# A residual with a conditioned relu layer: W loaded in rows of 4p + k over 128 partitions, x turned in columns 4p + k, W3 ahead of W2, and two instructions moved up

## The chip, the cores and the metric

The kernel runs on one core of one Trainium2 chip. The metric is the device time of one execution in microseconds. The kernel before took 111.57 us (median of three runs, 110.3 to 112.86).

## The reference

x is (4, 1024, 512) in float32, cond is (4, 256), W is (1536, 512), b is (512). Cut to what matters:

```
hidden = concatenate([cond, cond], axis=-1)                  # (4, 512)
x_mean = mean(x, axis=1)                                     # (4, 1, 512)
fused  = concatenate([x, x_mean, hidden], axis=-1)           # along the features, each row
out    = x + relu(fused @ W + b)
```

So with W cut into W1, W2, W3 of 512 rows each, out = x + relu(x @ W1 + bias of the batch), and that bias is mean(x) @ W2 + hidden @ W3 + b.

## The kernel before

**Data.** x is cut into eight groups g of 512 rows (two a batch). A group lies in `xa` with partition 32 j + m for row 32 lb + m and column quadrant j (128 columns). VectorE turns 32 x 32 blocks: `turn_x` (L288) takes the 32 columns 32 k to 32 k + 31 of each quadrant and writes block k of x transposed to a PSUM bank, 128 features by 512 rows. Partition 32 j + m of block k then holds feature 128 j + 32 k + m, and so W1's and W2's rows are loaded in that order, by one DMA for each 32 partitions.

**Three products for float32.** Each operand is split in two: ScalarE's `x_high` (L229) writes the rounded `xh` (and sums it over the rows into `xsum` in the same instruction), VectorE's `x_low` (L300) subtracts it from the PSUM bank to give `xl`. `w1_high` (L225, ScalarE) and the loop at L198 (POOL) do the same for W1, giving `w1h` and `w1l`. TensorE adds w1h xh, w1h xl and w1l xh over the four blocks k. A tile (g, t) is one quarter t of the output features for one group: 12 products of 512 columns into one of four PSUM banks `ps_y`. `n` numbers the tiles. Two banks `ps_xt` hold turned pieces, so `turn_x(n)` waits for `x_low(n - 2)`.

**Group 0** is done in two halves of 256 rows, block by block, as W1 lands. Its and group 1's products are copied by ScalarE's `save` (L237) to `relu_t`, since no bias is there yet.

**The bias.** `mean_terms(b)` (L317, VectorE) adds the sums of the two groups and makes `w2x`, W2's four blocks each times its part of the sum: one multiplication (L328), three multiply-adds (L331). `mean_bias(b)` (L421, TensorE) sums `w2x` over partitions into `ps_mean`. `sum_bias(b)` (L341, VectorE) adds the constant row and turns it into `bias`. The constant comes from `w3sum` on POOL (L210), 8 small products (two records each in the trace, L471), and `const_row` (L372).

**Output.** ScalarE's `relu(n)` (L242) adds the bias and applies relu, VectorE's `turn_back(n)` (L306) turns it into `back`, POOL adds it to `xa` (`residual`, L204), SP stores the group (L190). The last group is added by VectorE in half tiles.

**Orders written out by hand.** Each engine's list is in program order. ScalarE: `x_high(0)`, `x_high(1)`, `w1_high(0)`, `w1_high(1)`, then pairs, `x_high` to piece 10, `save(0)`, `x_high(11)`, more saves; and from relu 8 on, one `x_high` behind each relu. VectorE: group 1 and 2 are turned and split, `mean_terms(0)`, the constant row, `sum_bias(0)`, group 3, `mean_terms(1)`, then for each tile n its `turn_back(n)`, and from n = 4 on a `turn_x` and an `x_low` of the group three ahead. TensorE: group 0, tiles (1, 0) to (1, 3), constant, `mean_bias(0)`, tiles (2, 0) to (2, 3) with `mean_bias(1)` in the middle of (2, 3), then a loop over pairs of groups with the next `mean_bias` behind t = 2 of the second.

**Queues.** SP issues nearly all DMAs in order; ScalarE issues half of those of x's first group and of W1, at the start. In SP's list the order is: x's group 0 first half (two of four), W1 block 0, block 1, blocks 2 and 3 (two DMAs each), x's group 0 second half (two), cond (four), x's groups 1 and 2, W2 (four), W3 (two), b (four), then x's groups 3 to 7.

Of the kernel before, what the change touches and what calls it, by code (L numbers as in the profile page):

```python
# [24 lines left out]
P = 128  # L25
Q = 32
NQ = P // Q
# [5 lines left out]
XT_BANKS = 2  # L33
# [7 lines left out]
def build(nc, x, cond, w, bvec, out):  # L41
# [7 lines left out]
    assert D == NK * P and D == NQ * NK * Q and H == 2 and w.shape == (3 * D, D) and 2 * C == D  # L49
    assert NK % XT_BANKS == 0 and NK == Y_BANKS == BACK_RING and RELU_RING == H * NK  # L50

# [22 lines left out]
    ov = out.rearrange("b (h lb lm) (j e) -> (b h) j lm lb e", h=H, lm=Q, j=NQ)  # L74
    wv = w[0:2 * D, :].rearrange("(s j k m) o -> s j m k o", s=2, j=NQ, m=Q)

# [9 lines left out]
    with ExitStack() as ctx:  # L86
# [62 lines left out]

        def load_w1(eng, first, end, quadrants):  # L150
            for j in quadrants:
                eng.dma_start(w1[Q * j:Q * j + Q, first:end], wv[0, j, :, first:end]).then_inc(w1_landed[first], 16)  # L152

        def load_w2(eng, quadrants):
            for j in quadrants:
                eng.dma_start(w2[Q * j:Q * j + Q], wv[1, j]).then_inc(w2_landed, 16)

# [10 lines left out]
        @block.sync  # L168
        def _(sp):
            load_x0(sp, 0, LOW)  # L170
            load_w1(sp, 0, 1, LOW)
            load_w1(sp, 1, 2, LOW)
            load_w1(sp, 2, NK, LOW)
            load_x0(sp, 1, LOW)
            sp.wait_ge(cond_zeroed, 1)
            for j in range(NQ):
                sp.dma_start(cond_c[Q * j:Q * j + B], cv[j].rearrange("b (m k) -> b m k", k=CK)).then_inc(cond_landed, 16)  # L177
            load_x(sp, 1, ORDER)
            load_x(sp, 2, ORDER)
            load_w2(sp, ORDER)  # L180
            for r in range(2):
                sp.dma_start(w3[:, r], w3v[r]).then_inc(w3_landed, 16)
            for j in range(NQ):
                sp.dma_start(b_row[Q * j:Q * j + Q], bvec[P * j:P * j + P].partition_broadcast(Q)).then_inc(b_landed, 16)
            for g in range(3, G):
                load_x(sp, g, ORDER)
            for g in range(LAST):
                sp.wait_ge(added, NK * (g + 1))
                for j in ORDER:
                    sp.dma_start(ov[g, j], xa[Q * j:Q * j + Q, g]).then_inc(stored, 16)  # L190
            store_last(sp, range(0, 2))
            sp.wait_ge(stored, 16 * (NQ * LAST + 2 * NQ))

        @block.gpsimd
        def _(pool):
            nc.gpsimd.memset(cond_c[:], 0.0).then_inc(cond_zeroed, 1)

            for k in range(NK):  # L198
                pool.wait_ge(w1_landed[min(k, NK - 2)], 16 * NQ)
                pool.wait_ge(w1h_ready, k + 1)  # L200
                nc.gpsimd.tensor_tensor(as_tiles(w1l[:, k]), by_tile(w1[:, k]), as_tiles(w1h[:, k]),  # L201
                                        ALU.subtract).then_inc(w1l_ready, 1)
# [13 lines left out]
        def _(act):  # L216
            load_x0(act, 0, HIGH)
            act.wait_ge(ones_set, 1)
            nc.scalar.activation(act_warm[:], ones[:, 0:1], ACT.Relu)
            load_w1(act, 0, 1, HIGH)  # L220
            load_w1(act, 1, 2, HIGH)
            load_w1(act, 2, NK, HIGH)
            load_x0(act, 1, HIGH)

            def w1_high(k):  # L225
                act.wait_ge(w1_landed[min(k, NK - 2)], 16 * NQ)
                nc.scalar.activation(as_tiles(w1h[:, k]), by_tile(w1[:, k]), ACT.Copy).then_inc(w1h_ready, 1)  # L227
# [26 lines left out]

            x_high(0)
            x_high(1)
            w1_high(0)
            w1_high(1)
            for k in range(2, NK):
                x_high(k)  # L260
                w1_high(k)
            for n in range(NK, pieces_to(H) - 1):
                x_high(n)
            save(0)
            x_high(pieces_to(H) - 1)
            for n in range(1, NK):
# [19 lines left out]
        def _(dve):  # L286

            def turn_x(n):  # L288
                g, l, nl, k = pieces[n]
                if k == 0:  # L290
                    if g == 0:
                        dve.wait_ge(x0_landed[l // HL], 16 * NQ)
                    else:
                        dve.wait_ge(x_landed[g], 16 * NQ)
                if n >= XT_BANKS:
                    dve.wait_ge(xl_ready, n + 1 - XT_BANKS)
                nc.vector.transpose(ps_xt[:, n % XT_BANKS, 0:nl],  # L297
                                    xa[:, g, l // Q:(l + nl) // Q, Q * k:Q * k + Q]).then_inc(xt_ready, 1)

# [17 lines left out]
            def mean_terms(b):  # L317

                if b == 0:
                    nc.vector.tensor_tensor(xsum[:, 1], xsum[:, 0], xsum[:, 1], ALU.add).then_inc(halves_summed, 1)  # L320
                    dve.wait_ge(w2_landed, 16 * NQ)
                    dve.wait_ge(halves_summed, 1)
# [56 lines left out]
            for n, (g, l, nl, t) in enumerate(tiles):  # L379

                if n % NK == 0 and l == 0:
                    if n // NK % H == H - 1 and n // NK // H + 1 < B - 1:
                        sum_bias(n // NK // H + 1)
                    elif n // NK == H * (B - 1):
                        sum_bias(B - 1)
                turn_back(n)
# [145 lines left out]
```

## Time and profile before

| | us |
|---|---|
| median of three runs | 111.57 |
| the profiled execution | 109.98 |
| its span | 108.2 |
| PE busy | 97.4 |
| DVE (VectorE) busy | 85.4 |
| ACT (ScalarE) busy | 50.4 |
| POOL busy | 43.5 |

The granted TensorE clock was 0.996 of full speed over the span. The span runs from the first to the last instruction or transfer; the profiled execution's time has 1.8 us more around it. Times in the rows are in microseconds from the start of the span. An instruction's busy time may overlap the next one's, since engines pipeline. The idle time in brackets is that of the engine just before the instruction, with what ended it. DMA moved 20.08 MB, 186 GB/s in the mean.

### The profile page before, as it was taken

How to read it: one execution, taken by the hardware profiler on the slowest of the kernel's cores; microseconds unless marked ns; L12 is line 12 of the kernel's file. 1: busy time of each engine (PE TensorE's matmuls, PEld its weight loads, DVE VectorE, ACT ScalarE, POOL GpSimd, SP SyncE). 2: the span in 40 equal slices, each digit the busy share in tenths (PEclk: the TensorE clock that was granted, in tenths of full speed). 3: DMA queues.
4: the chain of work that ended last, by engine and by line, in shares of the span. 5: the costliest groups of instructions: out<-in, count | busy, mean ns of one | idle time of the engine just before them, and what ended most of it. 6: DMA issues, size and time to landing. Idle time of an engine off the chain costs nothing.

```text
span 108.2 us, 1750 instructions
## 1 busy us (share of the span) xinstructions
PE 97.4 (90%) x542; PEld 79.7 (74%) x542; DVE 85.4 (79%) x149; ACT 50.4 (47%) x122; POOL 43.5 (40%) x38
## 2 busy tenths in 40 slices
PE   5969999799969999489999999999999999999900
PEld 2349999688847886278888886888888868999900
DVE  1263869998997999999999955999999967796630
ACT  3185416985225991287396002873950008322210
POOL 1039500000440000999856400488564199960000
PEclk9999999999999999999999999999999999999998
DMA  2999999999999999999886194000861930969956
GB/s 71 276 291 264 227 226 230 243 250 333 220 220 222 222 222 222 226 224 263 244 204 186 33 236 126 0 0 0 210 178 41 241 106 0 217 181 230 245 126 171
DMA packets 35719, 20.08 MB, mean 186 GB/s; under 512 B 1536, under 2 KB 34432, under 8 KB 35712
## 3 DMA queue, kind: packets, MB, share of 16 engines
q1 hardware_dynamic: 33184, 18.42, 76.9%
q10 hardware_dynamic: 2528, 1.57, 5.4%
q8 instruction: 3, 0.05, 0.2%
q14 instruction: 4, 0.03, 0.1%
HBM read 11.60 MB, written 8.39 MB: 185 GB/s over the span
## 4 chain that ended last, share of the span: by engine, by line
PE 53%; DVE 18%; ACT 10%; DMA 7%; SPq 6%; issue 2%; ACTq 0%; DVEq 0%
PE ps_y L406 52%; DMA xa<-in_x_dram 7%; DVE w2x L331 6%; ACT xh L234 5%; ACT relu_t L252 3%; DVE ps_xt L297 3%; DVE xl L303 3%; DVE back L314 3%; SPq L152 2%; SPq L144 2%; ACT relu_t L239 1%; SPq L148 1%; SPq L177 1%; PE ps_mean L425 1%; DVE w2x L328 1%
## 5 line engine op out<-in xcount | busy, mean ns | idle before, releaser
L406 PE MATMUL ps_y<-xh,w1h 128*128 128x256 f32 (+2 forms) x160 | 52.9, 352 | 3.3 <-ACT relu_t L252 1.8
L406 PE MATMUL ps_y<-xl,w1h 128*128 128x256 f32 (+2 forms) x160 | 52.1, 347 | 0.0
L406 PE MATMUL ps_y<-xh,w1l 128*128 128x256 f32 (+2 forms) x160 | 51.9, 347 | 0.0
L206 POOL TENSOR_TENSOR xa<-xa,back 128x512 f32 x28 | 35.7, 1297 | 29.8 <-DVE back L314 29.8
L406 PEld LDWEIGHTS ps_y<-xh,w1h 128*128 128x128 f32 x160 | 28.7, 189 | 8.9 <-issue 3.2
L406 PEld LDWEIGHTS ps_y<-xh,w1l 128*128 128x128 f32 x160 | 28.7, 189 | 3.9
L406 PEld LDWEIGHTS ps_y<-xl,w1h 128*128 128x128 f32 x160 | 28.8, 189 | 3.6
L252 ACT ACTIVATE relu_t<-ps_y,bias 128x512 f32<-128x512 f32 (+1 forms) x28 | 17.3, 626 | 29.4 <-DVE bias L346 20.1
L234 ACT ACTIVATE xh<-ps_xt 128x512 fp32r<-128x512 f32 (+1 forms) x36 | 19.7, 548 | 14.9 <-DVE ps_xt L297 14.8
L297 DVE STREAM_TRANSPOSE ps_xt<-xa 128x512 f32<-128x512 f32 (+1 forms) x36 | 22.3, 642 | 5.1 <-DMA xa<-in_x_dram 4.7
L303 DVE TENSOR_TENSOR xl<-ps_xt,xh 128x512 fp32r<-128x512 f32 (+1 forms) x36 | 22.2, 617 | 4.6 <-ACT xh L234 4.6
L314 DVE STREAM_TRANSPOSE back<-relu_t 128x512 f32<-128x512 f32 (+1 forms) x36 | 22.1, 631 | 3.9 <-ACT relu_t L252 3.8
L331 DVE SCALAR_TENSOR_TENSOR w2x<-w,bsum,w2x 128x512 f32<-128x512 f32 x12 | 11.3, 938 | 0.4
L210 POOL TENSOR_TENSOR w3sum<-w 128x1024 f32<-128x1024 f32 x1 | 2.4, 2396 | 16.3 <-DMA w<-in_L_cond_W_dram 16.3
L201 POOL TENSOR_TENSOR w1l<-w,w1h 128x512 fp32r<-128x512 f32 x4 | 5.1, 1293 | 6.3 <-ACT w1h L227 6.2
L234 ACT ACTIVATION_READ_ACCUMULATOR xh<-ps_xt 128x1 f32 x36 | 7.1, 197 | 0.0
L252 ACT ACTIVATE relu_t<-relu_t,bias 128x512 f32<-128x512 f32 x8 | 5.4, 720 | 2.2 <-DVE bias L346 2.2
L239 ACT ACTIVATE relu_t<-ps_y 128x512 f32<-128x512 f32 x8 | 4.5, 596 | 3.7 <-PE ps_y L406 3.7
L403 PE MATMUL ps_mean<-warm 128*128 128x512 bf16 x14 | 5.0, 533 | 1.2 <-DVE warm L358 1.2
L339 DVE TENSOR_TENSOR xa<-xa,back 128x256 f32<-128x256 f32 x8 | 5.1, 633 | 0.3
L403 PEld LDWEIGHTS ps_mean<-warm 128*128 128x128 bf16 x14 | 1.7, 130 | 3.9 <-issue 2.4
L343 DVE SCALAR_TENSOR_TENSOR bias_row<-ps_mean,const_row 128x128 f32<-128x128 f32 x4 | 1.1, 281 | 3.3 <-PE ps_mean L425 3.3
(20 smaller groups left out, 14.2 us busy)
## 6 DMA issues: line engine op xcount, KB each, us to landing
xa<-in_x_dram SPq DMA_DIRECT2D x28, 256.0 KB, 6.8
out_dram<-xa SPq DMA_DIRECT2D x28, 256.0 KB, 4.0
w<-in_L_cond_W_dram SPq DMA_DIRECT2D x4, 256.0 KB, 7.2
w<-in_L_cond_W_dram SPq DMA_DIRECT2D x2, 512.0 KB, 10.4
xa<-in_x_dram SPq DMA_DIRECT2D x4, 128.0 KB, 3.9
xa<-in_x_dram ACTq DMA_DIRECT2D x4, 128.0 KB, 4.2
out_dram<-xa SPq DMA_DIRECT2D x4, 128.0 KB, 2.9
out_dram<-xa ACTq DMA_DIRECT2D x4, 128.0 KB, 2.4
```

What stands on the lines that cost most here:

```text
L201: nc.gpsimd.tensor_tensor(as_tiles(w1l[:, k]), by_tile(w1[:, k]), as_tiles(w1h[:, k]), ALU.subtract).then_inc(w1l_ready, 1)
L206: nc.gpsimd.tensor_tensor(rows, rows, back[:, t], ALU.add).then_inc(added, 1)
L234: nc.scalar.activation(xh[:, g % SLOTS, k, l:l + nl], ps_xt[:, n % XT_BANKS, 0:nl], ACT.Copy, accum_out=xsum[:, part, k:k + 1]).then_inc(x ...
L239: nc.scalar.activation(relu_t[:, n % RELU_RING], ps_y[:, n % Y_BANKS], ACT.Copy).then_inc(y_saved, 1)
L252: nc.scalar.activation(relu_t[:, slot, 0:nl], products, ACT.Relu, bias=bias[:, g // H, t, g // H:g // H + 1]).then_inc(relu_done, 1)
L297: nc.vector.transpose(ps_xt[:, n % XT_BANKS, 0:nl], xa[:, g, l // Q:(l + nl) // Q, Q * k:Q * k + Q]).then_inc(xt_ready, 1)
L303: nc.vector.tensor_tensor(xl[:, g % SLOTS, k, l:l + nl], ps_xt[:, n % XT_BANKS, 0:nl], xh[:, g % SLOTS, k, l:l + nl], ALU.subtract).then_i ...
L314: nc.vector.transpose(back[:, n % BACK_RING, 0:nl // Q], relu_t[:, n % RELU_RING, 0:nl].rearrange("p (lb om) -> p lb om", om=Q)).then_inc( ...
L331: nc.vector.scalar_tensor_tensor(out=w2x[:], in0=w2[:, k], scalar=bsum[:, k:k + 1], in1=w2x[:], op0=ALU.mult, op1=ALU.add).then_inc(w2x_st ...
L339: nc.vector.tensor_tensor(rows, rows, back[:, n % BACK_RING, 0:nl // Q], ALU.add).then_inc(last_added, 1)
L403: nc.tensor.matmul(ps_mean[:], warm[:, 0:P], warm[:], start=True, stop=True)
L406: return nc.tensor.matmul(ps_y[:, t, ls], lhs, rhs, start=start, stop=stop, skip_group_check=True)
```

## The change

- x's block k is no longer the 32 columns 32 k to 32 k + 31 of each quadrant, but every fourth one beginning at k. Partition 32 j + m then holds feature 4 (32 j + m) + k, that is 4 p + k. `turn_x` reads 32 floats with a step of four.
- With that, W1's and W2's rows are loaded as 4 p + k: one DMA for all 128 partitions where there were four. W1's three loads are all issued by SP, and so are all four of x's group 0, second half. ScalarE issues only its two of the first half. W2 is one DMA.
- W3 is loaded ahead of W2.
- ScalarE's order: `w1_high(0)` ahead of `x_high(1)`; `save(0)` ahead of `x_high(10)` as well.
- `sum_bias(1)` stands behind `turn_back(0)`, no longer behind `turn_back(3)`. The other batches' stay where they were.

```diff
-    wv = w[0:2 * D, :].rearrange("(s j k m) o -> s j m k o", s=2, j=NQ, m=Q)
+    wv = w[0:2 * D, :].rearrange("(s p k) o -> s p k o", s=2, k=NK)
...
-        def load_w1(eng, first, end, quadrants):
-            for j in quadrants:
-                eng.dma_start(w1[Q * j:Q * j + Q, first:end], wv[0, j, :, first:end]).then_inc(w1_landed[first], 16)
-
-        def load_w2(eng, quadrants):
-            for j in quadrants:
-                eng.dma_start(w2[Q * j:Q * j + Q], wv[1, j]).then_inc(w2_landed, 16)
+        def load_w1(eng, first, end):
+            eng.dma_start(w1[:, first:end], wv[0, :, first:end]).then_inc(w1_landed[first], 16)
...
             load_x0(sp, 0, LOW)
-            load_w1(sp, 0, 1, LOW)
-            load_w1(sp, 1, 2, LOW)
-            load_w1(sp, 2, NK, LOW)
-            load_x0(sp, 1, LOW)
+            load_w1(sp, 0, 1)
+            load_w1(sp, 1, 2)
+            load_w1(sp, 2, NK)
+            load_x0(sp, 1, ORDER)
...
             load_x(sp, 1, ORDER)
             load_x(sp, 2, ORDER)
-            load_w2(sp, ORDER)
             for r in range(2):
                 sp.dma_start(w3[:, r], w3v[r]).then_inc(w3_landed, 16)
+            sp.dma_start(w2[:], wv[1]).then_inc(w2_landed, 16)
...
-            load_w1(act, 0, 1, HIGH)
-            load_w1(act, 1, 2, HIGH)
-            load_w1(act, 2, NK, HIGH)
-            load_x0(act, 1, HIGH)
...
-            x_high(0)
-            x_high(1)
-            w1_high(0)
-            w1_high(1)
-            for k in range(2, NK):
+            for k in range(NK):
                 x_high(k)
                 w1_high(k)
-            for n in range(NK, pieces_to(H) - 1):
+            for n in range(NK, pieces_to(H) - 2):
                 x_high(n)
             save(0)
+            x_high(pieces_to(H) - 2)
             x_high(pieces_to(H) - 1)
...
                 nc.vector.transpose(ps_xt[:, n % XT_BANKS, 0:nl],
-                                    xa[:, g, l // Q:(l + nl) // Q, Q * k:Q * k + Q]).then_inc(xt_ready, 1)
+                                    xa[:, g, l // Q:(l + nl) // Q, k:P:NK]).then_inc(xt_ready, 1)
...
-                if n % NK == 0 and l == 0:
-                    if n // NK % H == H - 1 and n // NK // H + 1 < B - 1:
-                        sum_bias(n // NK // H + 1)
-                    elif n // NK == H * (B - 1):
-                        sum_bias(B - 1)
+                if n == 1:
+                    sum_bias(1)
+                elif n == NK * (H + 1):
+                    sum_bias(2)
+                elif n == NK * H * (B - 1):
+                    sum_bias(B - 1)
                 turn_back(n)
```

The waits on `w1_landed` and `w2_landed` count one DMA (16) instead of four.

## Rows read from the trace of the kernel before

**Rows 1.** The page, part 1: busy us (share of the span), instructions.
```profile
PE 97.4 (90%) x542; PEld 79.7 (74%) x542; DVE 85.4 (79%) x149; ACT 50.4 (47%) x122; POOL 43.5 (40%) x38
```

**Rows 2.** Timeline from 0 us: start, us, engine, instruction, count [idle before, releaser].
```profile
5.94 0.38 ACT L234 ACTIVATE xh<-ps_xt 128x256 fp32r<-128x256 f32 x1
...
6.29 1.40 ACT L227 ACTIVATE w1h<-w 128x512 fp32r<-128x512 f32 x2
...
7.07 0.71 PE L406 MATMUL ps_y<-xh,w1h 128*128 128x256 f32 x4 [0.89 <-ACT w1h L227]
```

**Rows 3.** Timeline, 15 to 21 us: group 1's pieces and the first save.
```profile
15.40 1.32 DVE L297 STREAM_TRANSPOSE ps_xt<-xa 128x512 f32<-128x512 f32 x2 [0.64 <-DMA xa<-in_x_dram]
...
17.68 0.28 PE L406 MATMUL ps_y<-xh,w1l 128*128 128x256 f32 x1
...
18.36 0.60 ACT L234 ACTIVATE xh<-ps_xt 128x512 fp32r<-128x512 f32 x1 [0.93 <-DVE ps_xt L297]
...
18.95 0.59 ACT L239 ACTIVATE relu_t<-ps_y 128x512 f32<-128x512 f32 x1
...
19.59 0.50 PE L406 MATMUL ps_y<-xh,w1h 128*128 128x512 f32 x1 [0.55 <-ACT relu_t L239]
...
20.42 0.69 DVE L303 TENSOR_TENSOR xl<-ps_xt,xh 128x512 fp32r<-128x512 f32 x1 [0.18 <-ACT xh L234]
```

**Rows 4.** Timeline of PE, 28 to 66 us: constant, mean_bias, tile (3, 0).
```profile
31.04 0.67 PE L471 MATMUL ps_const<-w3sum,cond_t 128*32 128x128 f32 x16 [0.28 <-POOL w3sum L210]
32.29 0.43 PE L425 MATMUL ps_mean<-w2x,ones 128*32 128x128 f32 x8 [0.58 <-DVE w2x L331]
...
42.40 0.43 PE L425 MATMUL ps_mean<-w2x,ones 128*32 128x128 f32 x8
...
46.25 0.50 PE L406 MATMUL ps_y<-xh,w1h 128*128 x1 [1.83 <-ACT relu_t L252]
...
65.51 0.42 PE L425 MATMUL ps_mean<-w2x,ones 128*32 128x128 f32 x8
```

**Rows 5.** Timeline of POOL, 24 to 60 us.
```profile
28.50 2.40 POOL L210 TENSOR_TENSOR w3sum<-w 128x1024 f32<-128x1024 f32 x1 [16.26 <-DMA w<-in_L_cond_W_dram]
```

**Rows 6.** Timeline of DVE, 24 to 66 us.
```profile
26.08 0.69 DVE L303 TENSOR_TENSOR xl<-ps_xt,xh 128x512 fp32r<-128x512 f32 x1 [0.18 <-ACT xh L234]
...
27.67 4.56 DVE L331 SCALAR_TENSOR_TENSOR w2x<-w,bsum,w2x 128x512 f32<-128x512 f32 x3
...
39.88 2.33 DVE L331 SCALAR_TENSOR_TENSOR w2x<-w,bsum,w2x 128x512 f32<-128x512 f32 x3
...
44.82 0.31 DVE L346 STREAM_TRANSPOSE bias<-bias_row 128x128 f32<-128x128 f32 x1
...
45.65 1.28 DVE L297 STREAM_TRANSPOSE ps_xt<-xa 128x512 f32<-128x512 f32 x2
...
61.46 2.33 DVE L331 SCALAR_TENSOR_TENSOR w2x<-w,bsum,w2x 128x512 f32<-128x512 f32 x3
```

**Rows 7.** Stretches: from:to, length, granted clock, DMA share, GB/s.
```profile
22.00:23.00 1.00, 1.00 1.08 242
...
25.00:26.00 1.00, 1.00 1.00 393
```

**Rows 8.** Timeline of ACT, 45 to 48 us.
```profile
45.25 0.69 ACT L252 ACTIVATE relu_t<-ps_y,bias 128x512 f32<-128x512 f32 x1 [4.27 <-DVE bias L346]
46.37 0.60 ACT L234 ACTIVATE xh<-ps_xt 128x512 fp32r<-128x512 f32 x1 [0.43 <-DVE ps_xt L297]
...
46.95 0.68 ACT L252 ACTIVATE relu_t<-ps_y,bias 128x512 f32<-128x512 f32 x1
```

**Rows 9.** Lines 364 and 346: durations min/median/max in ns, first and last start, form.
```profile
L364 DVE STREAM_TRANSPOSE cond_t<-cond_c x1: 233/233/233, 14.5 to 14.5; 128x64 f32<-128x64 f32 x1
...
L346 DVE STREAM_TRANSPOSE bias<-bias_row x4: 311/312/314, 33.2 to 88.7; 128x128 f32<-128x128 f32 x4
```

More of the change, by code:

```diff
@@ L49, in build @@
     assert D == NK * P and D == NQ * NK * Q and H == 2 and w.shape == (3 * D, D) and 2 * C == D
-    assert NK % XT_BANKS == 0 and NK == Y_BANKS == BACK_RING and RELU_RING == H * NK
+    assert B == 4 and NK % XT_BANKS == 0 and NK == Y_BANKS == BACK_RING and RELU_RING == H * NK
     pieces = [(0, l, HL, k) for l in (0, HL) for k in range(NK)]
@@ L198, in _ @@
             for k in range(NK):
-                pool.wait_ge(w1_landed[min(k, NK - 2)], 16 * NQ)
+                pool.wait_ge(w1_landed[min(k, NK - 2)], 16)
                 pool.wait_ge(w1h_ready, k + 1)
@@ L219, in _ @@
             nc.scalar.activation(act_warm[:], ones[:, 0:1], ACT.Relu)
-            load_w1(act, 0, 1, HIGH)
-            load_w1(act, 1, 2, HIGH)
-            load_w1(act, 2, NK, HIGH)
-            load_x0(act, 1, HIGH)
             def w1_high(k):
-                act.wait_ge(w1_landed[min(k, NK - 2)], 16 * NQ)
+                act.wait_ge(w1_landed[min(k, NK - 2)], 16)
                 nc.scalar.activation(as_tiles(w1h[:, k]), by_tile(w1[:, k]), ACT.Copy).then_inc(w1h_ready, 1)
@@ L320, in mean_terms @@
                     nc.vector.tensor_tensor(xsum[:, 1], xsum[:, 0], xsum[:, 1], ALU.add).then_inc(halves_summed, 1)
-                    dve.wait_ge(w2_landed, 16 * NQ)
+                    dve.wait_ge(w2_landed, 16)
                     dve.wait_ge(halves_summed, 1)
```

## Prediction, made before the change was run

> **What bounds the kernel now.** I read the busy times first, then PE's timeline with what ended each of its idle times, then the timelines of the engines named there, and last the DMA rates by stretch. TensorE is busy for 90% of the span, VectorE for 79% [rows 1]. So the time is what PE has to do plus its gaps. Its gaps before 46.25 us are: the start (first product at 7.07, released by the first `w1h` [rows 2]), 0.55 us before tile (1, 0) at 19.59, waiting for `save(0)` [rows 3], 0.28 us before the 16 constant products at 31.04 (for `w3sum`) and 0.58 us before `mean_bias(0)` at 32.29 (for `w2x`), and 1.83 us before tile (3, 0) at 46.25, waiting for a relu [rows 4]. After 46.25 PE has no gap until its last product, and then stores follow. Whatever is won before 46.25 therefore arrives at the end, if VectorE stays ahead; whatever VectorE falls behind by is lost.
>
> **Start: the order of `w1_high` and `x_high`.** ScalarE ran `x_high(1)` at 5.94 and the two `w1_high` from 6.29 [rows 2]. With `w1_high(0)` ahead of `x_high(1)`, it can begin 0.35 us sooner, if block 0 of W1 has landed. It is 256 KB in one transfer behind two of x, by one queue, where eight transfers had two queues. Gain between 0 and 0.35; I take 0.3, because the bytes ahead of it are the same. The following `w1_high(1)` ends when it did (the same three instructions stand before it). PE's first block of products is then not followed by a wait of more than about 0.05 us.
>
> **`save(0)` one `x_high` sooner.** PE's tile 0 ends with a product at 17.68 [rows 3]; `x_high(10)` at 18.36 stood ahead of `save(0)` at 18.95, and PE waited until 19.59. Now `save(0)` goes at about 17.6 to 18.2, in a hole of ScalarE's, and `x_high(10)` follows without delay. PE could start at 19.04 less 0.3, a gain of 0.85. But products of tile (1, 0) need `xl` of pieces 10 and 11, the latter subtracted from 20.42 to 21.11 [rows 3], and PE would want it at 18.75 + 3 x 0.68 = 20.8. That chain starts from x's group 1, which landed at 15.38; SP issues it 0.46 us sooner (one DMA less before it), and I give it 0.1 to 0.4. The gain behind tile (1, 0) is between 0.5 (nothing lands sooner) and 0.95; I take 0.7.
>
> **W3 ahead of W2.** In before, `w3sum` ran from 28.50, and the three multiply-adds of `w2x` took 4.56 us beside it, against 2.33 us where POOL is idle [rows 5, 6]. With W3 first, `w3sum` lies beside turns and subtractions with PSUM at one end; the four `w1l` on POOL lay beside such work at the start, with no stretch in it. The Trainium skill (SBUF — State Buffer, "SBUF: two separate sides") says that a DVE instruction with two SBUF inputs and a GpSimd instruction that reads SBUF exclude each other for a whole instruction. By that rule the trace agrees: 2.23 us lost beside a 2.40 us instruction.
>
> W2 now lands last, and `mean_terms(0)` may wait for it. Before, the pair had landed by 28.46, the start of `w3sum` less its delay [rows 5]. W2 over 32 partitions a transfer moved at 242 GB/s, W3 over 128 at up to 393 [rows 7]. The 1.05 MB of W2 at the second rate instead of the first take 2.7 us instead of 4.3: both have landed at 26.9, and at 26.5 with the sooner start. The bound from above is 28.46 (no faster), the one from below about 26. `mean_terms(0)` can begin its multiplications at 27.1, after `x_low(15)` (at 26.08 before, [rows 6]); all four take 0.5 + 2.33 us. `w2x` is done at 29.7, or 31.3 at the upper bound, not 32.24. PE gets there when tile 1 and the constants are through: 30.76 - 0.7 + 0.67 = 30.7. So PE's `mean_bias(0)` starts at 30.7, not 32.29: **gain 1.55**, and the wait for W2 has a cover of 1.0 us. At the upper bound the gain is 0.9; with no cover left each later microsecond of W2 costs one.
>
> **Batch 1's bias.** The turns, subtractions and `mean_terms(1)` take VectorE 9.97 us from the end of one `w2x` to the next (32.24 to 42.21, the end of the stretch at 39.88 [rows 6]); PE reaches `mean_bias(1)` 10.11 us after `mean_bias(0)` (32.29 to 42.40 [rows 4]). These stay tied. Before, four `turn_back` of 0.6 us then came ahead of `sum_bias(1)`, whose turn at 44.82 released the relu at 45.25, and that PE's tile (3, 0) at 46.25 [rows 4, 6, 8]. Now one stands ahead, and the sum waits for PE. What is queued behind that wait are `turn_back(1)` and on, for which only POOL and, later, ScalarE wait. Call PE's `mean_bias(0)` T. `mean_bias(1)` starts at T + 10.11; from such a start to the bias it took 1.22 us in batch 0 (32.29 to 33.51): bias at T + 11.33, the relu and PE's start 1.1 us later (45.14 to 46.25), T + 12.43. PE's tile (2, 3) ends at T + 12.13. Of the 1.83 us a stall of 0.3 remains.
>
> But the three turns pushed behind the bias are late next. ScalarE has `x_high(16)` between relu 8 and relu 9 (46.37 and 46.95 [rows 8]), and it waits for `turn_x(16)`, which VectorE runs after all `turn_back` to number 4 (45.65 [rows 6]). From bias to the end of relu 9 it was 2.4 us; three more turns make it 4.2, and with PE's delay 4.5. PE wants tile (3, 1) 1.1 + 2.75 = 3.85 after the bias: a new stall of 0.65. Net gain of this part: 1.83 - 0.3 - 0.65 = **0.9**. Bounds: 0.6 (POOL's ring also late) and 1.5 (PE's delay behind the relu hidden).
>
> **Later.** `w2x` of batch 2 was done at 63.8 (stretch at 61.46 [rows 6]), PE's `mean_bias(2)` came at 65.51 [rows 4]: cover 1.7. VectorE gains 1.55 (T) + 0.2 and loses 1.8 of shifted turns after the bias, PE gains 2.45, so 0.6 us of cover is left. Nothing else runs short. The DMA issues saved on ScalarE lie beside its table load and warm-up and cost nothing; `load_x0` of the second half moves whole to SP, 0.46 us each for four, behind three instead of six of W1, so it is issued at the same time. POOL's waits are only renumbered.
>
> **The stride.** `turn_x` now reads every fourth float. Nothing in the trace reads at a 16-byte step. The nearest is the turn of `cond_c` at a step of two floats: 64 elements in 233 ns, against 128 contiguous ones in 312 ns [rows 9], 1.2 ns an element between them, and a 512-element turn takes about 0.7 us, so it costs nothing at 8 bytes. I take nothing at 16 too, as the nearest row has it. The upper bound is the slowest rate of any streaming row, `w3sum` with 1024 elements in 2.40 us, 2.3 ns an element, twice that of a turn: 0.54 us on each of 28 full turns. The Trainium skill (SBUF — State Buffer, in "Door 1: The DMA port swizzle") speaks against my choice: lines are 16 bytes, and full bandwidth wants at least two accesses to a line. By it the cond turn (two a line) is free and this one (one a line) pays, at a price that the page does not give; no row here shows it.
>
> **Sum.** 1.55 + 0.9 = 2.45 us. The profiled execution took 109.98 us (span 108.2), so such a one would take 107.5 (span 105.8). It is the low one of three with median 111.57, from which the forecast is 109.1.
>
> **Rivals.** (a) *Turns at half rate*, the other side. Eight of them lie between x's groups 1 and 2 and `w2x`: +4.3 less 1.0 of cover, T at about 33.95, 1.65 later than before. Four more before `mean_bias(1)`: PE waits 2.0. Bias at T + 13.45, relu 9 later by one turn: tile (3, 1) 3.5 us later than before. Then eight per batch, +4.3, against 0.6 to 2.7 of cover: `mean_bias(2)` 6.6 later, `mean_bias(3)` and the end 8.3 later: 119.9. It decides from about 0.2 us a turn, where the gain is used up; at 0.27 (half as slow again) the same steps give 112.7. For it: the rule above; against it: the 8-byte row. (b) *W2's wait takes the place of W3's*: the 128-partition load is no faster, W2 lands at 28.46, T at 31.4, total gain 1.8: 109.8. Against it: 393 GB/s. (c) *No new stall at relu 9, and x lands sooner*: `x_high(16)` finds its turn in time or PE's stall is short, gain 3.4: 108.2. (d) *Nothing of the first 1.5 arrives*, because block 0 of W1 comes later over one queue: PE's start slips, but the wait for `w2x` absorbed it before and T moves by what is beyond 1.0 of cover; it is inside (b).
>
> **Chances.** The sum 0.48 (107.9 to 110.2 by its bounds), (b) with (d) 0.12, (c) 0.10, (a) at full price 0.22, at a part of it 0.08. A measurement of this kernel tells about 2% from no change, here 2.2 us, so the sum lies just beyond the border: 0.30 of its 0.48 is faster by more. Faster: 0.30 + 0.10 = 0.40. Same: 0.18 + 0.12 + 0.04 = 0.34. Slower: 0.22 + 0.04 = 0.26. The range goes from 107.0 (below (c)) to 118.5, which leaves out the dearer half of (a); the likeliest case's own range is 107.9 to 110.2.
>
> **What would show it.** Right: `turn_x` at 0.7 us per 512 elements; PE's gap before tile (1, 0) gone and small ones inside it; `w3sum` before 26 us and `w2x` multiply-adds at 2.33 us for three; `mean_bias(0)` near 30.7; the 1.83 us gap cut to 0.3 and a gap near 0.65 before tile (3, 1), released by a relu behind `x_high(16)`; span 105.8. Wrong: turns of 1.2 us and PE waiting for `xl` and `w2x` throughout; VectorE idle before `w2x` until W2 lands after 28; PE's first product later than 7.07.

## The result and the profile after

The changed kernel takes 113.77 us (median of four runs, 113.33 to 114.35), the kernel before 110.94 in the same comparison. The ratio is 1.028, with an interval of 1.018 to 1.038: it is slower, though the interval leaves open whether by more than 2%. Its profiled execution has a span of 112.6 us, against 108.2. Some executions of every kernel take 1 to 2% longer with nothing in the kernel to explain it: the ratios leave these out, but the traces of three kernels below are of such ones (110.13 us for the changed kernel without the step, 110.65 for W3 ahead of W2 alone, 111.19 for ScalarE's order alone), so a few tenths of a microsecond in these three decide nothing.

The page of the changed kernel, busy times, the chain that ended last, and the costliest lines of VectorE, beside [rows 1]:

```profile
PE 98.9 (88%) x542; PEld 79.3 (70%) x542; DVE 94.3 (84%) x149; ACT 50.7 (45%) x122; POOL 43.8 (39%) x38
...
DVE 64%; PE 11%; issue 7%; DMA 6%; SPq 4%; ACT 3%; DVEq 0%; ACTq 0%
...
L286 DVE STREAM_TRANSPOSE ps_xt<-xa 128x512 f32<-128x512 f32 (+1 forms) x36 | 34.5, 983 | 4.8 <-DMA xa<-in_x_dram 4.4
...
L320 DVE SCALAR_TENSOR_TENSOR w2x<-w,bsum,w2x 128x512 f32<-128x512 f32 x12 | 9.0, 752 | 0.4
```

The 36 turns of x have grown from 22.3 to 34.5 us of VectorE's time (L297 before, L286 now), while the multiply-adds of `w2x` gave 2.3 back. VectorE as a whole grew by 8.9 us (a total that counts overlapping instructions once). The chain that ended last was 53% TensorE and 18% VectorE before; it is now 64% VectorE.

PE's timeline, its first product, the `mean_bias` products and the gaps, beside [rows 2, 4]:

```profile
7.58 0.71 PE L396 MATMUL ps_y<-xh,w1h 128*128 128x256 f32 x4 [1.25 <-ACT w1h L219]
...
22.48 0.50 PE L396 MATMUL ps_y<-xh,w1h 128*128 128x512 f32 x1 [0.74 <-DVE xl L292]
32.43 0.66 PE L461 MATMUL ps_const<-w3sum,cond_t 128*32 128x128 f32 x16
33.46 0.43 PE L415 MATMUL ps_mean<-w2x,ones 128*32 128x128 f32 x8 [0.37 <-DVE w2x L320]
44.61 0.42 PE L415 MATMUL ps_mean<-w2x,ones 128*32 128x128 f32 x8 [0.98 <-DVE w2x L320]
46.86 0.49 PE L396 MATMUL ps_y<-xh,w1h 128*128 x1 [0.23 <-issue]
50.44 0.50 PE L396 MATMUL ps_y<-xh,w1h 128*128 x1 [0.58 <-ACT relu_t L244]
68.67 0.43 PE L415 MATMUL ps_mean<-w2x,ones 128*32 128x128 f32 x8 [1.62 <-DVE w2x L320]
...
91.01 0.42 PE L415 MATMUL ps_mean<-w2x,ones 128*32 128x128 f32 x8
```

and the last `mean_bias` in before:

```profile
87.86 0.43 PE L425 MATMUL ps_mean<-w2x,ones 128*32 128x128 f32 x8
```

Read the start times against those of before. PE is 0.5 us late at its first product, 1.2 at `mean_bias(0)` (32.29), 2.2 at `mean_bias(1)` (42.40), and only 0.6 at tile (3, 0) (46.25), because the 1.83 us gap there has become 0.23. Then it loses again: 3.2 us late at `mean_bias(2)` (65.51), and as much at `mean_bias(3)` (91.01, 87.86 before). Four of the seven gaps shown name VectorE's work (`xl`, `w2x`), and the relu of a fifth (50.44) stood behind an `x_high` that waited for a turn.

VectorE's timeline, the turns for group 1 and for group 4, and the last bias, beside [rows 3, 6]:

```profile
16.31 2.11 DVE L286 STREAM_TRANSPOSE ps_xt<-xa 128x512 f32<-128x512 f32 x2
...
48.03 2.04 DVE L286 STREAM_TRANSPOSE ps_xt<-xa 128x512 f32<-128x512 f32 x2
...
93.20 0.25 DVE L332 SCALAR_TENSOR_TENSOR bias_row<-ps_mean,const_row 128x128 f32<-128x128 f32 x1
```

Two turns take 2.11 us instead of 1.32, and 2.04 instead of 1.28. At the end four `turn_back` that VectorE is behind with (90.79 to 93.2) stand ahead of the last `sum_bias`, 2.2 us after the start of `mean_bias(3)`; in before it began 0.5 us after (88.35), and VectorE had been idle for it. The last add of VectorE begins at 107.46, 3.7 us after that of before (103.77), and the stores behind it take 0.7 us longer.

### The profile page after: what moved, and what is told of

The parts are those of the page before. It is cut to its first block, busy times and chain, and to the rows that moved or that the text cites. A ratio compares the mean times of both kernels' runs of the same rounds, so it can differ in the third digit from the quotient of the medians.

```text
span 112.6 us, 1738 instructions
## 1 busy us (share of the span) xinstructions
PE 98.9 (88%) x542; PEld 79.3 (70%) x542; DVE 94.3 (84%) x149; ACT 50.7 (45%) x122; POOL 43.8 (39%) x38
## 4 chain that ended last, share of the span: by engine, by line
DVE 64%; PE 11%; issue 7%; DMA 6%; SPq 4%; ACT 3%; DVEq 0%; ACTq 0%
DVE ps_xt L286 28%; DVE xl L292 13%; PE ps_y L396 10%; DVE back L303 10%; DVE w2x L320 7%; DMA xa<-in_x_dram 6%; SPq L145 2%; ACT xh L226 2%; DVE bsum L315 2%; DVE w2x L317 2%; SPq L152 1%; ACT relu_t L244 1%; DVE bias_row L332 1%; PE ps_mean L415 1%; DVE bias L335 1%
## 5 line engine op out<-in xcount | busy, mean ns | idle before, releaser
L286 DVE STREAM_TRANSPOSE ps_xt<-xa 128x512 f32<-128x512 f32 (+1 forms) x36 | 34.5, 983 | 4.8 <-DMA xa<-in_x_dram 4.4
L320 DVE SCALAR_TENSOR_TENSOR w2x<-w,bsum,w2x 128x512 f32<-128x512 f32 x12 | 9.0, 752 | 0.4
L415 PE MATMUL ps_mean<-w2x,ones 128*32 128x128 f32 x32 | 1.7, 284 | 3.0 <-DVE w2x L320 3.0
```

The lines of the kernel that those rows point to most:

```text
L286: nc.vector.transpose(ps_xt[:, n % XT_BANKS, 0:nl], xa[:, g, l // Q:(l + nl) // Q, k:P:NK]).then_inc(xt_ready, 1)
L320: nc.vector.scalar_tensor_tensor(out=w2x[:], in0=w2[:, k], scalar=bsum[:, k:k + 1], in1=w2x[:], op0=ALU.mult, op1=ALU.add).then_inc(w2x_st ...
```

## The experiments

Four edits had come together: the step of four floats in the turns, W's loads over 128 partitions by SP alone, the order on the queues and ScalarE, and `sum_bias(1)`. Theory A said that the step is what made it slower and the rest is a small gain.

### Orders alone

The kernel before with the order edits and nothing else.

```diff
-            load_w2(sp, ORDER)
             for r in range(2):
                 sp.dma_start(w3[:, r], w3v[r]).then_inc(w3_landed, 16)
+            load_w2(sp, ORDER)
...
-            x_high(0)
-            x_high(1)
-            w1_high(0)
-            w1_high(1)
-            for k in range(2, NK):
+            for k in range(NK):
...
-            for n in range(NK, pieces_to(H) - 1):
+            for n in range(NK, pieces_to(H) - 2):
                 x_high(n)
             save(0)
+            x_high(pieces_to(H) - 2)
...
+                if n == 1:
+                    sum_bias(1)
```

> The kernel before with only the orders changed: W3 ahead of W2, w1_high(0) ahead of x_high(1), save(0) ahead of x_high(10), sum_bias(1) behind turn_back(0). Turns read contiguous floats and W comes in the old DMAs on two queues. Theory A (the step of four floats in turn_x is what made the changed kernel slower, and the orders alone are a gain): turns stay at 0.7 us, W2 in four DMAs lands near 28.5, mean_bias(0) near 31.4 (0.9 sooner), the 1.83 us gap before tile (3, 0) falls to about 0.3 with a new one of 0.65 before tile (3, 1): in all 1.8 us faster than before, ratio 0.984. Rival B (the orders themselves cost: the turns pushed behind the bias and W2 landing last): no faster than before, ratio 1.00 or above, with PE idle for w2x or relu for as long as before.

Measured: 109.06 us, ratio 0.9875 (0.9805 to 0.9945). Faster, by 1.25% instead of 1.6%. PE's and VectorE's timelines:

```profile
28.98 0.16 DVE L323 TENSOR_TENSOR bsum<-xsum 128x4 f32<-128x4 f32 x1 [1.48 <-DMA w<-in_L_cond_W_dram]
...
29.70 2.33 DVE L328 SCALAR_TENSOR_TENSOR w2x<-w,bsum,w2x 128x512 f32<-128x512 f32 x3
```
```profile
32.08 0.43 PE L423 MATMUL ps_mean<-w2x,ones 128*32 128x128 f32 x8 [0.48 <-DVE w2x L328]
42.57 0.43 PE L423 MATMUL ps_mean<-w2x,ones 128*32 128x128 f32 x8 [0.29 <-DVE w2x L328]
44.81 0.49 PE L404 MATMUL ps_y<-xh,w1h 128*128 x1 [0.21 <-issue]
48.03 0.50 PE L404 MATMUL ps_y<-xh,w1h 128*128 x1 [0.21 <-ACT relu_t L252]
```

The multiply-adds no longer meet `w3sum` (2.33 us, 4.56 in [rows 6]), but VectorE now stands idle 1.48 us for W2, which landed just before 28.98. So `mean_bias(0)` moved by 0.2 us only. The rest of the gain is at tile (3, 0). And tile (3, 1) starts 3.22 us after (3, 0) where it was 2.85 (46.25 to 49.10 in before): the new stall behind relu 9 is there, at 0.4 to 0.5 us.

### The step alone

```diff
-    wv = w[0:2 * D, :].rearrange("(s j k m) o -> s j m k o", s=2, j=NQ, m=Q)
+    wv = w[0:2 * D, :].rearrange("(s j m k) o -> s j m k o", s=2, j=NQ, m=Q)
...
-                                    xa[:, g, l // Q:(l + nl) // Q, Q * k:Q * k + Q]).then_inc(xt_ready, 1)
+                                    xa[:, g, l // Q:(l + nl) // Q, k:P:NK]).then_inc(xt_ready, 1)
```

> The kernel before with only the step: turn_x reads every fourth float and the rows of W1 and W2 are loaded as 4p + k, by the same number of DMAs on the same queues. Theory A: each 512-element turn takes 1.1 us instead of 0.73, mean_bias(0) comes 1.5 us later than before, mean_bias(2) about 4.3 later, the end 4 to 5.5 later: ratio 1.04 to 1.05. Rival B (the step costs little here, since VectorE has cover; the loss in the changed kernel comes from the loads or the orders): ratio below 1.015.

Measured: 115.56 us, ratio 1.056 (1.049 to 1.064). This one edit costs about 6 us, more than the whole change lost. It also changes which rows of W each load brings, but W1's first DMA landed 3.2 us after its issue, as with the old rows (3.1 to 3.4 in the kernels that keep them), and the next experiment keeps the new rows and drops the step. PE's timeline:

```profile
34.84 0.43 PE L425 MATMUL ps_mean<-w2x,ones 128*32 128x128 f32 x8 [1.48 <-DVE w2x L331]
46.01 0.43 PE L425 MATMUL ps_mean<-w2x,ones 128*32 128x128 f32 x8 [0.95 <-DVE w2x L331]
49.90 0.50 PE L406 MATMUL ps_y<-xh,w1h 128*128 x1 [1.88 <-ACT relu_t L252]
...
69.95 0.43 PE L425 MATMUL ps_mean<-w2x,ones 128*32 128x128 f32 x8 [0.68 <-DVE w2x L331]
```

PE waits for `w2x` three times, 2.6, 3.6 and 4.4 us later than before. The two single results do not add up to the whole (1.056 and 0.9875 against 1.028). Two gaps that the orders bear on, 1.48 and 1.88 us here, are 0.37 and 0.23 us in the changed kernel, so the orders seem to give back more where the turns are slow. That is not shown by itself, since the changed kernel has the wide loads as well.

### The changed kernel without the step

Only the turns' columns go back to `Q * k:Q * k + Q`.

> The changed kernel with the turns reading 32 contiguous floats again. Its products pair rows of W with the wrong columns of x, so the output is not the reference's; the work on every engine is as in the changed kernel but for the step. Theory A: the turns fall back to 0.73 us and the kernel comes to 2.0 us below before (ratio 0.98), of the 2.45 us forecast 0.4 being lost because PE's first product starts at 7.58 instead of 7.07 when W1 comes over one queue. Rival C (the one-queue loads of W1 and of x's group 0 are a large part of the loss): it stays above before less 1 us, ratio 0.99 or more, with PE waiting in the first 13 us.

Measured: 108.62 us, ratio 0.989 (0.984 to 0.994). Without the step everything else in the change is a gain of 1.1%, half of my forecast. Theory A holds: with and without the step, all else equal, the ratio to before is 1.028 and 0.989, some 4.3 us apart. The other half of the forecast is looked for below. VectorE's wait for W2 and PE's `mean_bias(0)` in this kernel:

```profile
30.24 0.16 DVE L315 TENSOR_TENSOR bsum<-xsum 128x4 f32<-128x4 f32 x1 [1.26 <-DMA w<-in_L_cond_W_dram]
...
33.34 0.43 PE L415 MATMUL ps_mean<-w2x,ones 128*32 128x128 f32 x8 [0.82 <-DVE w2x L320]
```

### What a step costs

```diff
-                nc.vector.transpose(ps_xt[:, n % XT_BANKS, 0:nl],
-                                    xa[:, g, l // Q:(l + nl) // Q, Q * k:Q * k + Q]).then_inc(xt_ready, 1)
+                step = {3: 2, 4: 3, 5: 4}.get(g, 1)
+                cols = slice(k, k + (Q - 1) * step + 1, step) if step > 1 else slice(Q * k, Q * k + Q)
+                nc.vector.transpose(ps_xt[:, n % XT_BANKS, 0:nl],
+                                    xa[:, g, l // Q:(l + nl) // Q, cols]).then_inc(xt_ready, 1)
```

and in `mean_terms(b)` reads of W2 at steps of 2, 3 and 4 for b = 1, 2, 3.

> The cost of a step by itself. In the kernel before, turn_x reads groups 3, 4 and 5 at steps of 2, 3 and 4 floats (8, 12 and 16 bytes), and mean_terms reads W2 for batches 1, 2 and 3 at steps of 2, 3 and 4 floats. The wrong columns and rows are read, so the output is not the reference's; the counts of elements are unchanged. Theory A (a read of SBUF at 16 bytes or more from one element to the next is slower, below it is free): turns of 0.73 us at steps 1 to 3 and 1.1 us at step 4, and the multiply-adds slower at step 4 alone. Rival D (the cost grows with the step, or any step costs): turns at 2 and 3 floats lie between 0.73 and 1.1. Rival E (it belongs to the turning of 32 x 32 blocks, not to the read): multiply-adds take 0.75 us at every step.

The turns' durations in ns (min/median/max), the first row for groups 1 to 3 (steps 1 and 2), then group 4 (step 3), group 5 (step 4); and the multiply-adds at steps 2, 3 and 4:

```profile
L299 DVE STREAM_TRANSPOSE ps_xt<-xa x12: 684/726/728, 14.8 to 36.6; 128x512 f32<-128x512 f32 x12
...
L299 DVE STREAM_TRANSPOSE ps_xt<-xa x4: 849/866/896, 45.2 to 50.0; 128x512 f32<-128x512 f32 x4
...
L299 DVE STREAM_TRANSPOSE ps_xt<-xa x4: 1075/1082/1090, 53.2 to 58.5; 128x512 f32<-128x512 f32 x4
...
L338 DVE SCALAR_TENSOR_TENSOR w2x<-w,bsum,w2x x3: 751/751/753, 39.4 to 41.0; 128x512 f32<-128x512 f32 x3
...
L338 DVE SCALAR_TENSOR_TENSOR w2x<-w,bsum,w2x x3: 895/896/903, 62.9 to 64.7; 128x512 f32<-128x512 f32 x3
...
L338 DVE SCALAR_TENSOR_TENSOR w2x<-w,bsum,w2x x3: 1126/1128/1129, 83.3 to 85.7; 128x512 f32<-128x512 f32 x3
```

8 bytes cost nothing, 12 bytes 0.15 us on 512 elements, 16 bytes 0.36 to 0.38 us. The multiply-adds pay the same, so it is the read and not the turning (rival E falls). At 12 bytes it costs something too, which neither A nor D had as it is: free to 8, then growing.

### Where it is paid

One operand at a time is given a step of four floats, by views such as

```diff
+                    bank = bank.rearrange(part if g == 4 else whole, s=4)
+                    high = high.rearrange(part if g == 5 else whole, s=4)
+                    low = low.rearrange(part if g == 6 else whole, s=4)
                 nc.vector.tensor_tensor(low, bank, high, ALU.subtract).then_inc(xl_ready, 1)
```

> Where a step costs, one look; permuted elements are read or written, so the output is not the reference's, the counts are unchanged. In the kernel before: mean_terms reads W2 at steps of 8, 16 and 32 floats for batches 1, 2 and 3; x_low reads its PSUM operand at a step of 4 floats in group 4, its SBUF operand in group 5, and writes at that step in group 6; relu 4 of ScalarE reads at a step of 4 floats and relu 5 writes at it; POOL's add reads `back` at that step for t = 0 and 1. Known from e4_steps: a multiply-add over 512 elements takes 0.75 us at 4 and 8 bytes, 0.92 at 12, 1.12 at 16. If the cost is per line of 16 bytes that is fetched, it ends there: 1.12 us also at 32, 64 and 128 bytes. If it grows with the distance, more. If it is a property of SBUF as such, ScalarE's and POOL's reads are slower at 16 bytes too; if it is VectorE's own, they stay at 0.72 and 1.30 us. Writes: no row so far; I expect them free.

VectorE's subtraction with the step on its PSUM operand, on its SBUF operand, and on its result in SBUF (one row of each); the multiply-adds at steps of 8, 16 and 32 floats; ScalarE's relu at step 1 and, in the last row, with the step on the read (one) and on the write (one):

```profile
50.84 0.67 DVE L320 TENSOR_TENSOR xl<-ps_xt,xh 128x512 fp32r<-128x512 f32 x1
...
58.70 1.04 DVE L320 TENSOR_TENSOR xl<-ps_xt,xh 128x512 fp32r<-128x512 f32 x1
...
74.60 1.08 DVE L320 TENSOR_TENSOR xl<-ps_xt,xh 128x512 fp32r<-128x512 f32 x1
```
```profile
L354 DVE SCALAR_TENSOR_TENSOR w2x<-w,bsum,w2x x3: 1129/1147/1214, 40.6 to 43.0; 128x512 f32<-128x512 f32 x3
...
L354 DVE SCALAR_TENSOR_TENSOR w2x<-w,bsum,w2x x3: 1108/1108/1120, 64.8 to 67.1; 128x512 f32<-128x512 f32 x3
...
L354 DVE SCALAR_TENSOR_TENSOR w2x<-w,bsum,w2x x3: 1171/1175/1177, 88.3 to 90.7; 128x512 f32<-128x512 f32 x3
...
L263 ACT ACTIVATE relu_t<-relu_t,bias x6: 713/720/745, 33.3 to 41.5; 128x512 f32<-128x512 f32 x6
L263 ACT ACTIVATE relu_u<-relu_t,bias x2: 1232/1242/1253, 38.9 to 40.0; 128x512 f32<-128x512 f32 x2
```

In PSUM the step is free (0.67 us). In SBUF it is paid on a read (1.04) and on a write (1.08); I had expected the write to be free. It does not grow beyond 16 bytes (1.11 to 1.18 us at 32 to 128 bytes). ScalarE pays 0.52 us either way, POOL's add 0.26 (1.56 us where t is 0 or 1, 1.30 otherwise). So it belongs to SBUF as three engines reach it, not to VectorE alone. (Only VectorE's read of PSUM was tried, at this one step.)

The Trainium skill (SBUF — State Buffer, in "Door 1: The DMA port swizzle") says that SBUF is read in lines of 16 bytes and that two accesses to a line are needed for full speed. By that rule the trace agrees at 8 bytes (free) and at 16 (0.38 us more on 512 elements, and no more beyond); the same note says that one can stride 4 fp32 for free, and there the measurement decides: a step of 3 floats costs 0.15 us here and one of 4 floats 0.38.

### Why PE started late

`w1_high(0)` had been due at 5.94 and came at 6.81 in the changed kernel. First, all loads of W1 and of x's second half by SP, in the old form of four DMAs:

```diff
-            load_w1(sp, 0, 1, LOW)
-            load_w1(sp, 1, 2, LOW)
-            load_w1(sp, 2, NK, LOW)
-            load_x0(sp, 1, LOW)
+            load_w1(sp, 0, 1, ORDER)
+            load_w1(sp, 1, 2, ORDER)
+            load_w1(sp, 2, NK, ORDER)
+            load_x0(sp, 1, ORDER)
```

> The kernel of e1_orders (order edits alone, contiguous turns) with all loads of W1 and all of x's group 0, second half, issued by SP, still four DMAs of 32 partitions for each. It tells whether the late start of the changed kernel (W1's block 0 landed at 6.8, not by 5.94; first product 7.58, not 7.07) comes from the one queue or from the form over 128 partitions. If it is the one queue: first w1h after 6.6 with a wait on the DMA, and 0.3 to 0.8 us slower than e1_orders. If it is the form: block 0 has landed by 6.0 as in e1_orders, and the time is that of e1_orders within 0.3 us.

Second, the form over 128 partitions on two queues:

```diff
             load_w1(sp, 0, 1)
-            load_w1(sp, 1, 2)
-            load_w1(sp, 2, NK)
-            load_x0(sp, 1, ORDER)
+            load_w1(sp, 2, 3)
+            load_x0(sp, 1, LOW)
...
+            load_w1(act, 1, 2)
+            load_w1(act, 3, 4)
+            load_x0(act, 1, HIGH)
```

> The kernel of e3_after_step1 (the changed kernel with contiguous turns; its output is not the reference's, since rows of W meet the wrong columns of x), with the loads over 128 partitions split over two queues: SP issues W1's blocks 0 and 2, ScalarE 1 and 3, and each half of x's second half. If one queue is what made W1 late: block 0 by 6.2 and the whole 0.3 to 0.8 us faster than e3_after_step1. If it is the form over 128 partitions, block 0 still lands at 6.8 to 7.2 and the time stays within 0.3 us.

ScalarE's first `w1h`, in the changed kernel, with one queue and four DMAs, and with two queues and one DMA, the last with PE's first product and the stretch from 12 to 14 us (length, granted clock, DMA share, GB/s):

```profile
6.81 0.63 ACT L219 ACTIVATE w1h<-w 128x512 fp32r<-128x512 f32 x1 [1.06 <-DMA w<-in_L_cond_W_dram]
```
```profile
5.64 0.62 ACT L223 ACTIVATE w1h<-w 128x512 fp32r<-128x512 f32 x1
```
```profile
8.40 0.63 ACT L221 ACTIVATE w1h<-w 128x512 fp32r<-128x512 f32 x1 [2.90 <-DMA w<-in_L_cond_W_dram]
...
9.18 0.71 PE L398 MATMUL ps_y<-xh,w1h 128*128 128x256 f32 x4 [3.47 <-ACT w1h L221]
...
12.00:14.00 2.00, 0.50 1.21 225
```

It is the form. W1's first DMA of 64 KB over 32 partitions landed 3.1 to 3.4 us after its issue in every kernel that has it, on one queue or two; the one of 256 KB over 128 partitions after 5.1, 5.6 (the kernel without the step) and 6.7 us (two queues, later than I expected). The whole block of 256 KB counts, and in four DMAs on the same one queue it had landed by 5.64. It is not the rows either: the step alone has the new rows in the old form, and its first DMA took 3.2 us. Whether the size of the DMA or the count of partitions does it was not separated. What happens in these microseconds is not shown; the DMA engines moved 68 GB/s between 4 and 5 us with two queues of wide loads, 113 and 174 with one (without the step, and with it), 207 in before.

As whole kernels neither is better than its base. One queue with four DMAs each: 112.14 us, ratio 1.015 (0.998 to 1.032), some 3 us more than orders alone, outside what I expected: SP needs 5.56 us to issue the 12 loads of W1, and x's group 1 is first issued at 10.62, not at 6.84. Wide on two queues: ratio 0.994 (0.987 to 1.001) against 0.989 (0.984 to 0.994) on one, so not shown to be worse; one of its ten executions took 201.06 us, for which no cause is known. In its trace PE was idle for 3.47 us before its first product at 9.18, and the granted clock was 0.68 from 10 to 12 us and 0.50 (1.2 GHz) from 12 to 14, so its time has more in it than the landing.

The rule in the Trainium skill (DMA: Bandwidth & Descriptors, "Rules for kernel authors") to use one 128-partition transfer in place of two over halves stands there as advice on bandwidth, and for the rate later in the run it fits: over W3 and W2 it reached 430 GB/s in the kernel without the step, against 242 for W2 in four DMAs and 393 for W3 in before [rows 7]. W2 did not land sooner for it: its one DMA of 1 MB took 12.8 us from issue to landing, its four in orders alone 8.4 to 10.3. For the first operand that an idle engine waits for, the runs show the opposite of a gain.

### The parts of the orders, one by one

`sum_bias(1)` alone (diff as in orders alone, last lines):

> The kernel before with only sum_bias(1) moved behind turn_back(0). By the trace of e1_orders: PE's gap before tile (3, 0) falls from 1.83 to about 0.25 us, tile (3, 1) gets 0.45 us later, so 1.1 us faster than before, ratio 0.990. mean_bias(0) stays near 32.3. If the gap only moved to a later tile, ratio 1.00.

Measured: 109.77 us, ratio 0.986 (0.975 to 0.997). That is as much as all the orders together gave. PE's timeline:

```profile
32.83 0.67 PE L472 MATMUL ps_const<-w3sum,cond_t 128*32 128x128 f32 x16 [2.25 <-POOL w3sum L210]
...
45.65 0.49 PE L407 MATMUL ps_y<-xh,w1h 128*128 x1 [0.23 <-issue]
```

The gap before tile (3, 0) is gone. The wait for `w3sum` was 0.28 us in [rows 4] and is 2.25 here, though nothing ahead of it was changed, and `mean_bias(0)` starts at 33.27, not at 32.29. So the trace of before is one case of what that kernel does, and W3's landing is what varies.

W3 ahead of W2 alone:

> The kernel before with only W3 loaded ahead of W2. The three multiply-adds of w2x take 2.33 instead of 4.56 us, but mean_terms(0) waits for W2 until about 29, so w2x is done at 31.8 to 32.1 instead of 32.24: 0.2 to 0.4 us faster, ratio 0.997, against 1.55 us that the prediction gave to this and the start together. If W2 landed by 27 as I predicted: mean_bias(0) at 31.5, where PE gets there, and 0.8 us faster.

Measured: 110.92 us (median of four, 108.98 to 112.58) beside 110.71 for before, with no ratio: too few of them to show a gain or a loss. Its trace says why so little comes of it: VectorE waits 1.21 us for W2, landed just before 29.54, and `mean_bias(0)` starts at 32.64.

ScalarE's order alone:

> The kernel before with only ScalarE's order changed: w1_high(0) ahead of x_high(1), save(0) ahead of x_high(10). PE starts 0.3 us sooner and tile (1, 0) loses its gap, but mean_bias(0) still waits for w2x, which waits for nothing of this: PE idles up to 1.2 us longer there and the end stays, ratio 1.00. If PE's own progress set mean_bias(0), 0.7 us faster, ratio 0.993.

Measured: 111.12 us, ratio 0.997 (0.991 to 1.002): nothing, as expected. PE's timeline of this one:

```profile
6.68 0.71 PE L403 MATMUL ps_y<-xh,w1h 128*128 128x256 f32 x4 [0.31 <-ACT w1h L227]
...
32.56 1.11 PE L468 MATMUL ps_const<-w3sum,cond_t 128*32 128x128 f32 x16 [2.00 <-POOL w3sum L210]
```

PE starts 0.4 us sooner and waits 2.00 us for `w3sum` before the constant. Here W3 landed at 29.6 and `w3sum` met only the end of the multiply-adds, which took 2.33 us, while `w3sum` took 2.82; in the profile of before it landed at 28.46 and came among them, and they took 4.56. With W2 first PE gets `mean_bias(0)` at 32.3 to 33.4 in the traces (before, this one, `sum_bias(1)` alone), with W3 first at 32.1 to 32.6 (orders alone, relu 9 below, W3 alone). Loading W3 first may be worth a few tenths; no ratio shows it.

### Two versions meant to be faster

Relu 9 ahead of `x_high(16)`:

```diff
                 relu(n)
+                if n == H * NK:
+                    continue
                 for _n in range(1 if n < NK else steps_of_x(n, 2)):
                     x_high(n_x)
                     n_x += 1
+                if n == H * NK + 1:
+                    x_high(n_x)
+                    n_x += 1
```

> The kernel of e1_orders with relu 9 ahead of x_high(16) on ScalarE. By my reading of e1_orders, tile (3, 1) starts 3.22 us after (3, 0) where 12 products take 2.75, since relu 9 stands behind x_high(16), and that behind turn_x(16). If so: 2.75 us between the two tiles and 0.45 us off the end, against before a ratio near 0.983. If relu 10 or xl become late instead, the gap moves to a later tile and nothing is won.

Measured: 108.58 us, ratio 0.979 with a wide interval (0.947 to 1.010), so not shown to be faster than orders alone as a whole. In the trace the stall is gone: tile (3, 1) starts 2.86 us after (3, 0) (45.03 to 47.89), and from tile (3, 0) to `mean_bias(2)` it is 19.37 us (45.03 to 64.40), 19.76 in orders alone (44.81 to 64.57) and 19.26 in before.

The same with W2 first again and without `w3sum`: PE sums the halves of W3 in 16 products.

```diff
-            pool.wait_ge(w3_landed, 16 * 2)
-            nc.gpsimd.tensor_tensor(w3sum[:], w3[:, 0], w3[:, 1], ALU.add).then_inc(w3_added, 1)
...
-                for k in range(CK):
-                    last = nc.tensor.matmul(ps_const[Q * j:Q * j + Q, 0:P], cond_t[:, k], w3sum[:, k, P * j:P * j + P],
-                                            start=(k == 0), stop=(k == CK - 1))
+                for r in range(2):
+                    for k in range(CK):
+                        last = nc.tensor.matmul(ps_const[Q * j:Q * j + Q, 0:P], cond_t[:, k], w3[:, r, k, P * j:P * j + P],
+                                                start=(r == 0 and k == 0), stop=(r == 1 and k == CK - 1))
```

> A version meant to beat both: e7_relu9 (order edits and relu 9 ahead of x_high(16)) with W2 ahead of W3 again and without w3sum: PE sums both halves of W3 in 16 small products instead of 8. Then nothing of POOL lies beside w2x, and W2 has landed near 25.5, before VectorE needs it at 27. w2x done by 30.5, mean_bias(0) at 31.3 where PE gets there after 16 products, 0.8 to 1.0 us sooner than in e7_relu9: about 3 us below before, ratio 0.973. If the constant's wait for W3 (landed 28.5) or PE's own work is the limit instead, mean_bias(0) stays above 31.8 and the ratio above 0.98.

Measured: 109.1 us, ratio 0.988 (0.982 to 0.994). Faster than before, but no better than orders alone. `w2x` was done at 30.1, as hoped; PE's 16 constant products then took from 29.98 to 32.44, the last mixed with those of `mean_bias(0)`, more than three times the 0.67 us of eight, at a granted clock of 1.00. The bias sum began at 32.80, where it began at 32.65 in orders alone. Why 16 take so long is open.

## Why the prediction was wrong

**The step (the part "The stride").** This failed. I took its price as nothing, by a row at 8 bytes, and carried that to 16; it is 0.38 us on each full turn. The 8-byte row itself was read rightly (0.73 us, free). The bounds, 0 and 0.54, did hold the price, and rival (a) had the mechanism: PE late at `w2x` of batch 0 and again at 1 and 2. By my own break-even of 0.2 us a turn the sign followed from the price. The size of (a) was too high: between its 112.7 at 0.27 and 119.9 at 0.54, 0.38 stands at 115.6 by a straight line (an estimate), and 113.77 was measured. It had `mean_bias(3)` 1.7 us later still than `mean_bias(2)`, and there nothing was added (3.2 us late at both). That 113.77 lies inside the stated range, 107.0 to 118.5, is the work of (a) alone; the sum that I believed in pointed the other way. What I had wrong besides was the weight: 0.30 for (a) in all, though the one rule that I had cited spoke against my choice, and no row of the trace reached 16 bytes.

**W2's landing (term of "W3 ahead of W2").** I had 26.5, with 28.46 as the upper bound. It landed just before 28.98 in orders alone, 29.54 with W3 first alone and 30.24 in the changed kernel without the step. So the upper bound was too low: it came from one execution, and x's groups ahead of W2 came later (group 1 landed at 17.0 in the kernel without the step and at 16.1 in orders alone, against 15.38 in [rows 3]), which ate what the 430 GB/s gave. The cover of 1.0 us that I gave the wait for W2 did not exist (27.1 + 2.83 is 29.9, not 29.7, so even by my numbers it was 0.8); the wait came, as rival (b) says. Of 1.55 us at `mean_bias(0)`, 0.2 came in orders alone, and it was 1.0 us *later* in the traced execution of the changed kernel without the step (33.34).

**The start.** Predicted 0.3 us sooner, measured 0.5 later. "The bytes ahead of it are the same" was not the point: the form of the transfer was. ScalarE's order does give the 0.4 us where W1 comes in the old form (6.68), but nothing of it arrives behind the constant and `w2x`.

**Batch 1's bias.** Right: 1.83 us became 0.2 (0.3 predicted), the new stall at tile (3, 1) is there behind `x_high(16)`, at 0.4 to 0.5 instead of 0.65. Net 0.9 predicted; alone the edit gave 1.4% (0.3 to 2.5%), some 1.5 us. `x_high(16)` found its turn a little sooner than I counted.

**The sum.** 2.45 us of gain were predicted without the step. The changed kernel without it is 1.1% faster, 1.2 us, and the bias alone gives that much. So even with the step free, the forecast would have been twice what came, because the 1.55 us at `mean_bias(0)` were not there.

## What to carry to other kernels

Before an operand is given a step, ask whether it lies in SBUF and how far apart its elements come: up to 8 bytes was free here, 12 bytes cost a fifth more and 16 bytes half as much again on every VectorE instruction of 512 float32. The engine that reads pays this each time, while the load that the step makes easier runs once. A row at half the step is no evidence for the whole one: where the Trainium skill names a condition that the row meets and the change does not, cost that case first.

A load in fewer, wider DMAs moved more GB/s in bulk here and came later for the first operand. When one load is moved ahead of another on a full queue, the last byte of the two lands no sooner (28.46 before, 28.98 to 29.54 after): look at who waits for the last one. And one trace is one execution: the wait for `w3sum` was 0.28 us in one kernel's trace and 2.25 us in that of a kernel with the same work up to there.

## What the runs showed of the hardware

- Float32 in SBUF, 512 elements, VectorE: 0.73 us a turn at 4 and 8 bytes from one element to the next, 0.87 at 12, 1.08 at 16. A multiply-add: 0.75, 0.75, 0.90, 1.13, and 1.11 to 1.18 at 32, 64 and 128. A subtraction: 0.67, and 1.04 with a read or 1.08 with the write at 16 bytes; its read of PSUM at that step is free (0.67).
- At 16 bytes ScalarE pays more than VectorE (0.72 to 1.24 us, read or write), POOL less (1.30 to 1.56, one read of two).
- One DMA of 256 KB over 128 partitions, first on its queue after x's two, landed 5.1 to 6.7 us after issue; 64 KB over 32 partitions 3.1 to 3.4.
- In the one trace where PE had 3.47 us without a product before its first one (at 9.18), the granted clock was 1.00 to 10 us, 0.68 from 10 to 12 and 0.50 (1.2 GHz) from 12 to 14; after 1.85 us without one (the changed kernel without the step) it stayed at 1.00.
